# Second experts' stage: rows written indirectly to their tokens' places as each expert ends, read back by plain transfers

## What is computed

```
logits = xf @ router_w
probs = jax.nn.softmax(logits, axis=-1)
w, idx = lax.top_k(probs, K)                        # K = 2 of E = 16
keep = myrank < capacity                            # rank of a token among those of its expert
w = jnp.where(keep, w, 0.0)
xe = x_pad[dispatch]                                # each expert's list of tokens
hidden = jax.nn.silu(xe @ gate_w) * (xe @ up_w)
out = (hidden @ down_w) * wbuf
combined = zeros.at[dispatch].add(out)              # back to token order
h = h + combined[:T]
```

## Time and profile before

| | |
|---|---|
| median of 3 runs | 1912.69 us (1912.63 to 1914.46) |
| the profiled execution's own time | 1919.82 us |
| its span | 1917.6 us |
| this stage's experts, first fetch to last `me_yb` | 982.9 to 1118.8 us of the span |
| its end, last `me_yb` to last addition to `h` | 1118.8 to 1163.1 us of the span |
| mean granted TensorE clock, share of full speed | 0.873 |

### The profile page before, as it was taken

How to read it: one execution, slowest core, us unless ns; L and a number is a source line. 1 busy time by engine, 2 the same in 40 slices (tenths; PEclk the granted TensorE clock), 3 DMA queues, 4 the chain that set the end, 5 groups by cost and what they waited for, 6 DMA issues and landing times. The chain is left out here.

```text
span 1917.6 us, 23877 instructions
## 1 busy us (share of the span) xinstructions
PE 1480.0 (77%) x8469; PEld 1176.7 (61%) x8469; DVE 1389.4 (72%) x2362; ACT 837.3 (44%) x1624; POOL 593.1 (31%) x409
## 2 busy tenths in 40 slices
PE   3898456499999667877569925975878799779797
PEld 3586335499996323443459924963367689566697
DVE  7576897996656599999447725878974567676676
ACT  5466653465544755555115504741233333423332
POOL 1500001322200199999134143356031231100320
PEclk9988678799999888989769967888978989869899
DMA  4410101111001303120437321003513010310110
GB/s 100 105 35 4 43 1 53 50 45 45 1 1 41 142 17 124 60 80 0 161 59 213 99 62 36 23 11 80 157 37 98 26 34 9 87 25 1 42 34 26
DMA packets 65313, 108.77 MB, mean 57 GB/s; under 512 B 34750, under 2 KB 43549, under 8 KB 63583
## 3 DMA queue, kind: packets, MB, share of 16 engines
q1 hardware_dynamic: 57218, 92.96, 16.5%
q0 software_dynamic: 6416, 9.29, 2.5%
q10 hardware_dynamic: 1562, 5.00, 0.9%
HBM read 83.82 MB, written 18.13 MB: 53 GB/s over the span
## 5 line engine op out<-in xcount | busy, mean ns | idle before, releaser
L2725 PE MATMUL c_pc<-c_st,ident 128*128 128x407 f32 x384 | 161.5, 571 | 49.2 <-POOL c_st L2689 42.8
L2681 POOL TENSOR_TENSOR c_dbub<-s_dub,s_bcb 128x814 f32<-128x814 f32 x96 | 171.3, 1813 | 80.5 <-POOLq L47 70.7
L2664 ACT ACTIVATE c_da<-s_deltab,s_ab 128x407 f32<-128x407 f32 x192 | 108.1, 594 | 115.7 <-DVE c_st L2769 96.3
L2725 PEld LDWEIGHTS c_pc<-c_st,ident 128*128 128x128 f32 x384 | 79.1, 213 | 129.4 <-POOL c_st L2689 59.1
L2765 DVE TENSOR_TENSOR_SCAN c_da<-c_da,c_dbub 128x814 f32<-128x814 f32 x60 | 110.6, 1843 | 2.5 <-ACT c_da L2668 2.5
L2183 ACT ACTIVATE e_sg<-e_pu,e_b 128x444 f32<-128x444 f32 (+1 forms) x96 | 56.7, 590 | 80.3 <-PE e_pu L2109 74.7
L3454 DVE SCALAR_TENSOR_TENSOR dc_acc<-dc_pp,dc_cw,dc_acc 128x1311 f32<-128x1311 f32 x48 | 75.9, 1584 | 21.6 <-ACT dc_acc L3371 20.2
L2264 DVE TENSOR_TENSOR e_sg<-e_sg,e_gate 128x444 f32<-128x444 f32 (+1 forms) x96 | 54.6, 570 | 48.2 <-ACT e_sg L2183 45.1
L2071 POOL TENSOR_TENSOR e_wlb<-e_wb,e_whb 128x1024 fp32r<-128x1024 f32 x16 | 42.1, 2655 | 126.0 <-ACT e_whb L2158 126.0
L2953 POOL DMA_INDIRECT me_xe<-m_xs,mt_rowsb x48 | 48.6, 1013 | 77.6 <-DVE mt_rowsb L3119 37.0
L3672 POOL TENSOR_TENSOR do_msb<-do_msb,d_half 111x8 f32<-111x8 f32 x11 | 27.7, 2519 | 140.9 <-DVE do_msb L3933 140.9
(11 more groups left out here) (698 smaller groups left out, 4669.1 us busy)
## 6 DMA issues: line engine op xcount, KB each, us to landing
s_bcb<-s_bc SPq DMA_DIRECT2D x48, 407.0 KB, 3.8
m_wb<-in_m_w SPq DMA_DIRECT2D x16, 768.0 KB, 8.5
e_wb<-in_e_w SPq DMA_DIRECT2D x4, 2048.0 KB, 7.9
m_ys<-me_yb SPq DMA_DIRECT2D x16, 384.0 KB
d_z<-d_first ACTq DMA_DIRECT2D x11, 384.0 KB, 2.7
d_first<-d_z SPq DMA_DIRECT2D x11, 384.0 KB, 3.5
le_wb<-in_l_w_e SPq DMA_DIRECT2D x9, 384.0 KB, 3.0
de_wb<-in_d_w_e SPq DMA_DIRECT2D x8, 384.0 KB, 3.0
```

The lines of the kernel that those rows point to most:

```text
L2664: last = nc.scalar.activation(da[k % 2][:, c * CH:(c + 1) * CH], delta[:, t, c0 + c, :], ACT.Exp, scale=a[:, n, c0 + c:c0 + c + 1])
L2681: nc.gpsimd.tensor_tensor(wide(dbu[k % DB][:, :]), du[:, t, c0:c0 + HC, :], bc[n][:, 0:1, :].broadcast_to([P, HC, CH]), ALU.mult).then_inc ...
L2725: last = nc.tensor.matmul(pc[:, c, 0:CH], ident[:, :], st[k % YB][:, c * CH:(c + 1) * CH], start=False, stop=(n == N - 1), skip_group_chec ...
```

## The change

After it, each expert's result goes indirectly to its tokens' places. `m_ys` is now two arrays of 1222 rows one behind the other, for the first and the second choice, each in token order with one spare row ahead, and behind them 768 rows for slots that hold no token. DVE makes the list of places `mt_destb` out of the same PSUM tile as `mt_rowsb`, with five small instructions behind it; two small ones that made the old list go. GpSimd issues three indirect stores of 128 rows for each expert (`scatter(e)`), behind the evict of it, and in GpSimd's program the fetch of expert e+4 now stands ahead of scatter(e) and behind scatter(e-1). The 22 fetches at the end go. In their place SP and ACT read `m_ys` back in token order with six plain transfers each (`back`), when all scatters have landed.

As a token without a kept choice is written by nobody, the first 2688 rows of `m_ys` are zeroed beforehand from the zeroed `me_yb` by one transfer of SP, and row 0 of `m_xs`, a new row that empty slots point at, by another. GpSimd's first fetch and DVE's first two evicts wait for these. SP no longer stores experts, so its refills of weight buffers wait for `me_split` alone. Two constant tables take the place of one (`m_offs`, `m_unused` for `m_base`).

```diff
@@ -2800,7 +2800,7 @@
 PASS, CAP = 124, max(1, math.ceil(B * S * 2 / 16 * 1.25))
-SLOTS = 384
+ZERO, YROWS = 3 * P * 7, 3 * P * 9
 def pool_dma_sems(nc, stack, names):
@@ -2828,15 +2828,15 @@
     CW = J * PASS
-    iota, base, sel, ranks, token = tables
+    iota, offs, unused, sel, ranks, token = tables
         s = sems(nc, stack, "mt_x_out mt_logit_mm mt_v mt_max mt_exp mt_hot mt_turned mt_rank mt_rank_mm mt_ids mt_m8 "
-                            "mt_idx mt_match mt_table_mm mt_table mt_table_turned mt_rows mt_slots mt_spare "
+                            "mt_idx mt_match mt_table_mm mt_table mt_table_turned mt_rows mt_dest "
                             "me_hi me_split me_xt_mm me_xh me_xl me_up_mm me_act me_prod me_high me_low me_down_mm "
-                            "me_y me_zero me_half me_sum me_y_out0 me_y_out1")
+                            "me_y me_zero me_zeroed me_half me_sum " + " ".join(f"me_back{n}" for n in range(len(GROUPS))))
         g = pool_dma_sems(nc, stack, " ".join(f"me_x{b}" for b in range(XB)) + " "
-                          + " ".join(f"me_g{t}" for t in range(NT)))
+                          + "me_out0 me_out1")
@@ -2853,8 +2853,8 @@
         rows = sb("mt_rowsb", [P, J, E], U32)
-        slot = sb("mt_slotb", [TT, NT, 2])
-        slot_idx = sb("mt_slot_idx", [TT, NT, 2], U32)
+        where = sb("mt_whereb", [P, J, E])
+        dest = sb("mt_destb", [P, J, E], U32)
@@ -2875,6 +2875,16 @@
         def slots(j):
             return slice(j * PASS, (j + 1) * PASS)
+        def back(eng, k):
+            for b in range(2):
+                eng.wait_ge(g[f"me_out{b}"], E // 2 * J * 16)
+            for n, (a, b) in enumerate(GROUPS):
+                for lo, hi in ROWS:
+                    at = k * (T + 1) + 1
+                    eng.dma_start(yg[k][lo:hi, a:b, :],
+                                  d["ys"][at:at + T].rearrange("(t p) n -> p t n", p=TT)[lo:hi, a:b]
+                                  ).then_inc(s[f"me_back{n}"], 16)
+
         @block.sync
         def _(sp):
             def weights(e):
@@ -2882,20 +2892,19 @@
                     sp.wait_ge(s["me_split"], e - RB + 2)
                 sp.dma_start(w[e % RB][:, :], w_dram[e]).then_inc(w_in[e % RB], 16)
-            def store(e):
-                sp.wait_ge(s["me_y"], e + 2)
-                sp.dma_start(d["ys"][e * SLOTS:(e + 1) * SLOTS, :].rearrange("(p j) n -> p j n", j=J),
-                             y[e % 2][:, :, :]).then_inc(s[f"me_y_out{e % 2}"], 16)
-
             for lo, hi in ROWS:
-                sp.dma_start(d["xs"].rearrange("(t p) n -> p t n", p=TT)[lo:hi], x[lo:hi, :, :]
+                sp.dma_start(d["xs"][1:T + 1].rearrange("(t p) n -> p t n", p=TT)[lo:hi], x[lo:hi, :, :]
                              ).then_inc(s["mt_x_out"], 16)
             for e in range(LEAD, RB):
                 weights(e)
-            for e in range(E):
-                if e + RB < E:
-                    weights(e + RB)
-                store(e)
+            sp.wait_ge(s["me_zero"], 4)
+            sp.dma_start(d["xs"][0:1, :], y[0][0:1, 0, :]).then_inc(s["me_zeroed"], 16)
+            sp.dma_start(d["ys"][0:ZERO].rearrange("(p a j) n -> p a (j n)", p=P, j=J),
+                         y[0][:, :, :].rearrange("p j n -> p (j n)").unsqueeze(1).broadcast_to([P, ZERO // (P * J), J * D])
+                         ).then_inc(s["me_zeroed"], 16)
+            for e in range(RB, E):
+                weights(e)
+            back(sp, 0)
         @block.scalar
         def _(act):
@@ -2939,6 +2948,7 @@
                     high(e + 1, f)
                 if 0 <= e and e + 3 < E:
                     high_weights(e + 3)
+            back(act, 1)
         @block.gpsimd
         def _(pool):
@@ -2955,19 +2965,24 @@
                         in_offset=bass.IndirectOffsetOnAxis(ap=rows[:, j, e:e + 1], axis=0)
                         ).then_inc(g[f"me_x{e % XB}"], 16)
+            def scatter(e):
+                if e == 0:
+                    pool.wait_ge(s["mt_dest"], 2)
+                pool.wait_ge(s["me_y"], e + 2)
+                for j in range(J):
+                    nc.gpsimd.indirect_dma_start(
+                        out=d["ys"], out_offset=bass.IndirectOffsetOnAxis(ap=dest[:, j, e:e + 1], axis=0),
+                        in_=y[e % 2][:, j, :], in_offset=None).then_inc(g[f"me_out{e % 2}"], 16)
+
             pool.wait_ge(s["mt_x_out"], 33)
+            pool.wait_ge(s["me_zeroed"], 33)
             pool.wait_ge(s["mt_rows"], 2)
+            for e in range(XB):
+                fetch(e)
             for e in range(E):
-                fetch(e)
-            pool.wait_ge(s["mt_slots"], 2)
-            for b in range(2):
-                pool.wait_ge(s[f"me_y_out{b}"], E // 2 * 16 + 1)
-            for t in range(NT):
-                for k in range(2):
-                    nc.gpsimd.indirect_dma_start(
-                        out=yg[k][:, t, :], out_offset=None, in_=d["ys"],
-                        in_offset=bass.IndirectOffsetOnAxis(ap=slot_idx[:, t, k:k + 1], axis=0)
-                        ).then_inc(g[f"me_g{t}"], 16)
+                if e + XB < E:
+                    fetch(e + XB)
+                scatter(e)
         @block.tensor
         def _(pe):
@@ -3004,7 +3019,7 @@
                 if e:
                     pe.wait_ge(s["me_xl"], e + 1)
                 else:
-                    pe.wait_ge(s["mt_rows"], 2)
+                    pe.wait_ge(s["mt_dest"], 2)
                 for j in range(J):
                     for k in range(KC):
                         last = nc.tensor.transpose(pt[:, k, slots(j)], xe[e % XB][0:PASS, j, k * P:(k + 1) * P],
@@ -3091,8 +3106,6 @@
                                     hot[:, :, :, :].rearrange("p t k e -> p t (k e)"),
                                     token[:, :].unsqueeze(2).broadcast_to([TT, NT, 2 * E]), ALU.mult
                                     ).then_inc(s["mt_ids"], 1)
-            link(nc.vector.scalar_tensor_tensor(slot[:, :, :], pick[:, :, :], float(SLOTS),
-                                                base[:, :].unsqueeze(1).broadcast_to([TT, NT, 2]), ALU.mult, ALU.add))
             for n, (a, b) in enumerate(GROUPS):
                 dve.wait_ge(s["mt_turned"], n + 2)
                 last = nc.vector.tensor_copy(hotT[:, a * TT:b * TT], turned[n][0:2 * E, 0:(b - a) * TT])
@@ -3110,14 +3123,19 @@
             dve.wait_ge(s["mt_table_mm"], 2)
             nc.vector.tensor_copy(table[:, 0:2 * CAP], pt[0:E, 0, 0:2 * CAP]).then_inc(s["mt_table"], 1)
-            link(nc.vector.scalar_tensor_tensor(slot[:, :, :], rank[:, :, :], float(CAP), slot[:, :, :], ALU.min,
-                                                ALU.add))
-            nc.vector.tensor_copy(slot_idx[:, :, :], slot[:, :, :]).then_inc(s["mt_slots"], 1)
             link(nc.vector.scalar_tensor_tensor(w2[:, :, :], rank[:, :, :], float(CAP), m8[:, :, 0:2], ALU.is_le,
                                                 ALU.mult))
             dve.wait_ge(s["mt_table_turned"], 2)
             nc.vector.tensor_copy(rows[0:PASS, :, :].rearrange("p j e -> p (j e)"), pt[0:PASS, 1, 0:J * E]
                                   ).then_inc(s["mt_rows"], 1)
+            ids_at = pt[0:PASS, 1, 0:J * E].rearrange("p (j e) -> p j e", e=E)
+            link(nc.vector.tensor_copy(where[96:P, :, :], unused[96:P, :, :]))
+            link(nc.vector.scalar_tensor_tensor(where[0:PASS, :, :], ids_at, 0.0, unused[0:PASS, :, :], ALU.is_equal,
+                                                ALU.mult))
+            link(nc.vector.tensor_tensor(where[0:PASS, :, :], ids_at, where[0:PASS, :, :], ALU.add))
+            link(nc.vector.tensor_tensor(where[0:PASS, :, :], where[0:PASS, :, :],
+                                         offs[0:PASS, :].unsqueeze(2).broadcast_to([PASS, J, E]), ALU.add))
+            nc.vector.tensor_copy(dest[:, :, :], where[:, :, :]).then_inc(s["mt_dest"], 1)
             def low_weights(e):
                 dve.wait_ge(s["me_hi"], e + 2)
@@ -3144,7 +3162,9 @@
             def evict(e):
                 dve.wait_ge(s["me_down_mm"], e + 2)
                 if e >= 2:
-                    dve.wait_ge(s[f"me_y_out{e % 2}"], e // 2 * 16 + 1)
+                    dve.wait_ge(g[f"me_out{e % 2}"], e // 2 * J * 16)
+                else:
+                    dve.wait_ge(s["me_zeroed"], 33)
                 nc.vector.tensor_copy(y[e % 2][0:PASS, :, :].rearrange("p j n -> p (j n)"), po[0:PASS, 0:J * D]
                                       ).then_inc(s["me_y"], 1)
@@ -3167,7 +3187,8 @@
                     low_weights(e + 3)
             def first(t):
-                dve.wait_ge(g[f"me_g{t}"], 32)
+                n = max(k for k in range(len(GROUPS)) if GROUPS[k][0] <= t)
+                dve.wait_ge(s[f"me_back{n}"], 4 * 16 + 1)
                 nc.vector.scalar_tensor_tensor(h[:, t, :], yg[0][:, t, :], w2[:, t, 0:1], h[:, t, :], ALU.mult, ALU.add
                                                ).then_inc(s["me_half"], 1)
```

(17 more changed lines are left out.)

## The result

| | before | after |
|---|---|---|
| median of 15 runs each, us | 1914.46 (1911.69 to 1922.13) | 1907.89 (1901.21 to 1912.56) |
| ratio | | 0.9968 (95% interval 0.9956 to 0.9980) |
| the profiled execution's own time, its span | 1919.8, 1917.6 | 1912.56, 1910.7 |
| mean granted TensorE clock | 0.873 | 0.876 |

The change makes the kernel 0.32% faster, some 6 us. The forecast was 13 us. The direction holds and the time lies in the range, by 0.1 us in the narrower of the two that are given (1893 to 1908; the other is 1889 to 1912), but half of the gain is missing. The ratio is taken from all runs, and isn't the quotient of the two medians.

What follows compares the result with a forecast made beforehand. The stage's end was taken as bound by a train of indirect fetches, and the rounds after the change by POOL. 23.6 gained at the end less 1.0 and 9.6 gave 13.0 us off, 1899.7 from 1912.7; range 1889 to 1912.

Steps and rivals of the forecast that it cites:

- the narrower of the two: Whole kernel: the main case's own range, 1893 to 1908, with the slow read at its worse end; chance 0.55.
- The start: First experts: refills 8 to 10 beside the first fetches delay their landing; +1.0 us, bounds 0 and +3.
- Among the experts: Expert rounds: POOL's six transfers and waits take 8.6 us against 7.45, delaying PE's last turn by 9.6.
- the mechanism: Expert rounds: POOL transfers begun while DVE runs `me_wl` or `me_hl` wait for its end; 1.1 us a round.
- The end: After the last expert: scatters, plain reads and additions take 20.7 us in place of 44.3, gaining 23.6.
- POOL does not keep up: Expert rounds: denies the rival that POOL keeps up, hardly any transfer waiting; 22.2 us off, 1890.5; chance 0.2.
- the second rival: Expert rounds: a scatter costs POOL 1.66 us or the queue is slower; round 9.8, no change, 1912.7; chance 0.16.
- The clock did fall: Expert rounds: rival that PE's clock falls in its waits; four such rounds cost 21.6 us, 1921.3; chance 0.09.

Runs made afterwards that it cites:

- gated: Kernel after, with SP's refills 9 to 15 held until the expert eight or nine before is evicted; 1901.62 us, ratio 0.9922 to the kernel before.
- three buffers: Kernel after, with refills 9 to 15 held back, fetches six ahead and three `me_yb`; 1893.76 us, again 1890.89, ratios 0.9889 and 0.9881 to the kernel before.
- two: Kernel after, with refills 9 to 15 held back and fetches six ahead, still two `me_yb`; 1911.76 us, again 1900.11, ratios 0.9936 and 0.9916 to the kernel before.

## Why the prediction came out half right

**The start was mis-sized: +1.0 forecast with a bound of 3, +4.0 measured.** The step said that refills 8 to 10 go beside the first fetches and that "a part falls after 994", and took a small share of their time. By the prediction's own figures those two refills are 5.4 us of all engines; the second turn came 4.5 us late, so most of the 5.4 came to bear and not a small part. The earlier trace rows already shows that the fetches by themselves take 96.7% of the engines while they move only 82 GB/s, which leaves little room beside them; the step didn't use that. The fetches' longest landing is 10.0 us, where the earlier trace rows has 8.3, and in the first ten microseconds the fetches moved 0.40 MB, half of what they move beside a single refill (0.73 before, 0.76 gated). Undoing the refills takes 6.1 us off the start, and doing them alone in the kernel before puts 4.2 on it. Before, a store that had to wait for expert 0 stood between them and the first fetches. The change took it away as if it had held nothing up.

**Among the experts the mechanism was right, and the size nearly: +9.6 forecast, +11.2 measured.** POOL's ten rounds were forecast at 8.6 and took 8.85. A round without the collisions is 7.69, not 7.50, since a scatter is 0.99 in the median and not 0.95 and a fetch behind a scatter up to 0.99. The collisions cost 1.17 a round, forecast 1.0 and 0.1: one is 1.06 in the mean, and there are eleven in ten rounds. From the end of expert 1's evict (1024.47) to the last start of fetch 15 (1112.11) it took 87.6, forecast 84.8; the landing behind it, to the turn at 1116.05, took 3.9, forecast 5.2. The difference is +1.6 (the kernel with gated refills takes 92.4 for the same stretch, this one 91.6). From expert 7 to 15 the turns are 8.85 apart in the mean, single ones 6.9 to 10.3; 8.6 was forecast. What each part weighs is shown by two runs: without `me_wl` on DVE no transfer is over 1.27 us, and with the fetch ahead of the scatter PE doesn't wait for rows. The Trainium skill (SBUF — State Buffer, Who interferes with whom) has an instruction of DVE with two inputs in SBUF contend with GpSimd where that reads SBUF, and infers that such a one does not stall the generation of a transfer. For the indirect ones, which read a list, the rule holds here and the inference doesn't, for scatters as for fetches. It holds one way only: all 16 `me_wl` took 1.75 to 1.76, also where a transfer was under way. That the reading of the list is the reason is not shown, as no other kind of transfer was begun inside `me_wl`.

**The end was right: 23.6 forecast, 22.4 measured.** The last scatter's landing was over-estimated: the reads are issued 2.5 after its start, where 3.6 were taken. The reads were under-estimated: the first group needs 6.5 from its issue, forecast 5.0, and the second came 1.7 later than forecast. Between the two 0.91 MB took 4.05 us, 224 GB/s, where 292 was taken. The two errors have opposite signs, so that 22.4 is so near is in part luck. The Trainium skill's fit (DMA: Bandwidth & Descriptors, Anatomy of one DMA), which the prediction sets beside it, is made there for transfers that GpSimd issues; by it the first group would be there 4.1 after the issue, and these transfers of SP and ACT needed 6.5.

**The sum.** 1.2 less at the end, 3.0 more at the start and 1.6 more in the rounds, 0.3 of which was caught up by the last evict, make 5.5 of 13.0. That is what is missing in the profiles (7.5). The step that failed is thus first the start, put at +1.0 where +4.0 came, and next the length of a round, put at 8.6 where it was 8.85. The upper end of the range, 1908, is less than its own bounds give: 16 - 1 - 14.6 is 0.4 off, 1912, the end of the wider one.

**The rivals.** POOL does not keep up. A scatter isn't slower than a fetch by more than 0.03, so the second rival's price of 1.66 is off. The clock did fall: the turn behind a wait for rows of 2.74 took 1.50, and the window from 1070 to 1076 has 0.64. The last turn, behind a wait of 2.12, took 1.48. But the turn behind a wait of 2.69 took only 0.85, so the length of the wait alone doesn't decide.

```profile
1055.54 0.85 PE L3025 MATMUL me_pt<-ident,me_xe 124*128 124x124 f32 x6 [2.69 <-DMA me_xe<-m_xs,mt_rowsb]
...
1072.53 1.50 PE L3025 MATMUL me_pt<-ident,me_xe 124*128 124x124 f32 x6 [2.74 <-DMA me_xe<-m_xs,mt_rowsb]
...
1116.05 1.48 PE L3025 MATMUL me_pt<-ident,me_xe 124*128 124x124 f32 x6 [2.12 <-DMA me_xe<-m_xs,mt_rowsb]
```

It cost the chain nothing that can be seen: at the first of these turns POOL had no gap, and POOL set the time; the last turn is behind the last fetch, and from there to the last evict it took 21.0, before 21.3.

The first evict comes 1.6 us later with three buffers than with two (24.6 and 23.0), although the first two turns come at the same time. PE's granted clock is the difference. From 14 to 17 us after the first fetch it is 1.00 (2.4 GHz) with two buffers, and PE does 19 matmuls; with three it is 0.50 (1.2 GHz), and PE does 11:

```profile
997.32:1000.32 3.00, 3.00 (x19) 3.00 (x19) 0.96 (x3) 1.60 (x3) 2.39 (x3) 1.00 0.75 92
...
995.33:998.33 3.00, 3.00 (x11) 3.00 (x10) 0.52 (x2) 1.17 (x2) 2.39 (x3) 0.50 0.71 86
```

Three profiles with three buffers have it so. Why the clock rises later in them stays open.
